# The slots stage of a twelve-stage decoder: units interleaved over three rounds, two projections merged, the fixed state's products made once

## The reference, cut to what matters

```python
S = slot_init * slot_scale                       # the same 64 x 128 state for every batch
h = gelu(concat([x, mean(S)]) @ w1.T + b1)
route_logits = (h @ w2.T + b2) / (abs(tau) + 0.1)
topk_vals, topk_idx = top_k(route_logits, 8)
alpha = one_hot(topk_idx) * softmax(topk_vals)   # tokens x 64, eight not zero
gi = (alpha.T @ x) / (alpha.sum(over tokens) + 1e-8)
xr, xz, xn = split(gi @ gru_wih.T + gru_bih); hr, hz, hn = split(S @ gru_whh.T + gru_bhh)
r, z, n = sigmoid(xr + hr), sigmoid(xz + hz), tanh(xn + r * hn)
S_new = (1 - z) * n + z * S
out = (alpha @ (S_new @ wv.T + bv)) @ wo.T + bo
```

## Time and profile before

| what | value |
|---|---|
| median of three runs | 3283.29 us (3280.67 to 3284.57) |
| the profiled execution, span | 3279.6 us |
| slots stage in it | 768.4 to 911.6 us |
| busy over the whole span | PE 83%, DVE 59%, ACT 42%, POOL 40% |

### The profile page before, as it was taken

How to read it: one execution, slowest core, us unless ns; L and a number is a source line. 1 busy time by engine, 2 the same in 40 slices (tenths; PEclk the granted TensorE clock), 3 DMA queues, 4 the chain that set the end, 5 groups by cost and what they waited for, 6 DMA issues and landing times. The chain is left out here.

```text
span 3279.6 us, 78499 instructions
## 1 busy us (share of the span) xinstructions
PE 2706.7 (83%) x31817; PEld 1927.4 (59%) x31817; DVE 1946.2 (59%) x5123; ACT 1386.3 (42%) x3116; POOL 1315.4 (40%) x1379
## 2 busy tenths in 40 slices
PE   6992566676675999799899987898979999978986
PEld 4551333344443777466799976565447777765665
DVE  6997999354554444466454444465766665645665
ACT  4552465354344555344322213554134444435544
POOL 3541566173211111444233333454643343424546
PEclk9996677787687999899799998898889999998998
DMA  3000000400000000100000000000000000000000
GB/s 104 3 2 1 1 1 1 114 1 1 1 7 33 1 2 2 41 3 3 8 1 1 1 1 4 14 2 33 12 6 2 2 2 2 2 8 2 2 2 26
DMA packets 25351, 37.33 MB, mean 11 GB/s; under 512 B 696, under 2 KB 22336, under 8 KB 24128
## 3 DMA queue, kind: packets, MB, share of 16 engines
q1 hardware_dynamic: 24992, 32.30, 3.2%
HBM read 30.07 MB, written 2.23 MB: 10 GB/s over the span
## 5 line engine op out<-in xcount | busy, mean ns | idle before, releaser
L1205 POOL TENSOR_TENSOR L_attn__qk<-L_attn__turned 128x512 f32<-128x512 f32 x128 | 161.6, 1274 | 303.5 <-DVE L_attn__turned L1316 303.5
L4316 PE MATMUL psum<-L_ffn__e_hT,weights 128*128 128x256 f32 x1024 | 245.1, 383 | 0.0
L787 DVE TENSOR_REDUCE L_xattn__nm<-psum 128x8 bf16<-128x1024 f32 x128 | 156.3, 1224 | 148.7 <-PE psum L982 142.3
L1316 DVE TENSOR_TENSOR L_attn__turned<-psum,weights 128x1024 f32<-128x1024 f32 x128 | 153.3, 1218 | 95.1 <-PE psum L1423 92.1
L4316 PEld LDWEIGHTS psum<-L_ffn__e_hT,weights 128*128 128x128 f32 x1024 | 187.0, 193 | 20.7
L4170 DVE TENSOR_TENSOR L_ffn__e_a<-L_ffn__e_sg,psum 128x512 f32<-128x512 f32 x128 | 87.9, 687 | 176.9 <-ACT L_ffn__e_sg L4162 176.8
L4162 ACT ACTIVATE L_ffn__e_sg<-psum 128x512 f32<-128x512 f32 x128 | 76.4, 597 | 259.1 <-PE psum L4316 259.1
L727 ACT ACTIVATE L_xattn__pT<-psum 128x1024 f32<-128x1024 f32 x128 | 124.0, 1021 | 58.0 <-PE psum L1010 58.0
L4329 PEld LDWEIGHTS psum<-weights,L_ffn__e_a 128*128 128x128 f32 x1024 | 134.4, 191 | 7.2 <-DVE L_ffn__e_a L4170 0.7
L1423 PE MATMUL psum<-L_attn__xT,weights 128*128 128x256 f32 x512 | 136.8, 401 | 2.0 <-DVE L_attn__turned L1316 1.3
L4329 PE MATMUL psum<-weights,L_ffn__e_a 128*128 128x128 f32 x1024 | 135.0, 275 | 0.5 <-DVE L_ffn__e_a L4170 0.5
(11 more groups left out here) (677 smaller groups left out, 7541.5 us busy)
## 6 DMA issues: line engine op xcount, KB each, us to landing
L_xattn__conv_toeplitz<-s4d_kernel SPq DMA_DIRECT2D x5, 1024.0 KB, 10.9
weights<-pack SPq DMA_DIRECT2D x1, 3328.0 KB, 10.3
weights<-pack SPq DMA_DIRECT2D x1, 3140.0 KB, 10.3
weights<-s4d_kernel SPq DMA_DIRECT2D x3, 1024.0 KB, 8.9
weights<-pack SPq DMA_DIRECT2D x1, 2370.0 KB, 9.3
out_dram<-X SPq DMA_DIRECT2D x8, 256.0 KB, 2.3
weights<-pack SPq DMA_DIRECT2D x1, 1732.5 KB, 14.4
ctxT<-ctxT_in SPq DMA_DIRECT2D x1, 1536.0 KB, 18.4
```

What stands on the lines that cost most here:

```text
L787: nc.vector.tensor_reduce(nm[:, n % 2, :].rearrange("p (g c) -> p g c", g=4)[:, 2 * u:2 * u + 2, 0:4], scores[u].rearrange("p g (i q) -> p ...
L1205: nc.gpsimd.tensor_tensor(qk[:, p % 2, u], turned[:, g % 2, :, 0:2 * P], turned[:, g % 2, :, 2 * P:4 * P], ALU.add).then_inc(qk_sb, 1)
L1316: nc.vector.tensor_tensor(turned[:, g % 2], proj[u % 2].unsqueeze(1).to_broadcast([P, 2, 4 * P]), k.w(name + "rope").rearrange("p (t q) -> ...
L4316: last = nc.tensor.matmul(bank[g % 2][:, 256 * c:256 * c + 256], k.w(name + w)[:, o:o + P], hT, start=True, stop=True)
```

## The change

Nothing outside `slots` changes but the packing of one weight (wv is stored unturned). The work is divided anew:

- The eight best of all units are chosen in the first part. sel now has a place for every unit, and `lowered` overwrites LG.
- The second part is 11 rounds; DVE does in one round the gates of unit i-1, weights of unit i+2, residual and norm of units i-2 and i-3, slot mean of unit i+1.
- The products of hsT with whh for the r and z gates, with the biases, are made once (gh_rz). DVE adds them to the accumulators in one new instruction for each unit, 128x512 (`gate_sum`, writes pre), and ACT makes th in one instruction of 128x512 from SBUF instead of two of 128x256 from PSUM.
- wv @ wo (wvo) and bv @ wo + bo are made once. `values` is one product of hnew with wvo; the svT copy is gone.
- `gather` sums over tokens with two matmuls instead of four.
- `with_bias(u)`, before the loop for unit 0, now follows `scaled` in its round.

The core of the diff:

```diff
-                pool.wait_ge(k.loaded[stage], 16)
-                with_bias(0)
-                lowered(0)
+                for u in range(UNITS):
+                    lowered(u)
                 scaled(0)
-                for v in range(UNITS + 1):
...
+                scaled(1)
+                for i in range(UNITS + 2):
+                    if unit(i - 1):
+                        difference(i - 1)
+                    if unit(i + 2):
+                        scaled(i + 2)
+                    if unit(i):
+                        with_bias(i)
+                    if unit(i - 2):
+                        root(i - 2)
...
                 def gates(u):
-                    act.wait_ge(gx_ps, u + 1)
+                    act.wait_ge(pre_sb, u + 1)
...
-                    for c in range(2):
-                        last = nc.scalar.activation(th[:, c, :], RZ[:, 4 * NS * c:4 * NS * c + 4 * NS], ACT.Tanh,
-                                                    bias=half_b[:, c:c + 1], scale=0.5)
-                    last.then_inc(th_sb, 1)
+                    nc.scalar.activation(th[:], pre[:], ACT.Tanh, scale=0.5).then_inc(th_sb, 1)
...
+                for i in range(UNITS + 3):
+                    if unit(i - 2):
+                        values(i - 2)
+                    if unit(i - 1):
+                        gates(i - 1)
+                    if unit(i):
+                        turned_mean(i)
+                    if unit(i - 1):
+                        candidate(i - 1)
+                    if unit(i - 3):
+                        block_out(i - 3)
+                    if unit(i + 1):
+                        turned_alpha(i + 1)
+                    if unit(i + 3):
+                        exponentials(i + 3)
...
+                nc.vector.tensor_copy(bv_cols[:], k.w(name + "bv").to_broadcast([P, P])).then_inc(bv_sb, 1)
...
+                def merged():
+                    dve.wait_ge(merged_ps, 1)
+                    nc.vector.tensor_copy(wvo[:], MERGED[:, 0:DM]).then_inc(merged_sb, 1)
+                    nc.vector.tensor_tensor(bo[:], MERGED[:, DM:2 * DM], k.w(name + "bo"), ALU.add).then_inc(merged_sb, 1)
...
+                def gate_sum(u):
+                    dve.wait_ge(gx_ps, u + 1)
+                    if u >= 1:
+                        dve.wait_ge(th_sb, u)
+                    nc.vector.tensor_tensor(pre[:].rearrange("p c (j n) -> p c j n", j=4),
+                                            RZ[:].rearrange("p (c j n) -> p c j n", c=2, j=4),
+                                            gh_rz[:].unsqueeze(2).to_broadcast([P, 2, 4, NS]), ALU.add).then_inc(pre_sb, 1)
...
-                        rz = RZ[:, 4 * NS * c:4 * NS * c + 4 * NS]
-                        nc.tensor.matmul(rz, k.w(name + "whh")[:, P * c:P * c + P],
-                                         hsT[:].unsqueeze(1).to_broadcast([P, 4, NS]), start=True, stop=False)
...
-                    nc.tensor.matmul(SV[:, 0:4 * NS], k.w(name + "wv"), hnew[:], start=True, stop=True).then_inc(svT_ps, 1)
-                    pe.wait_ge(svT_sb, u + 1)
...
                 gather(0)
-                for v in range(UNITS):
-                    state(v)
-                    if v + 1 < UNITS:
-                        gather(v + 1)
-                    values(v)
-                    spread(v)
+                for i in range(UNITS + 2):
+                    if unit(i):
+                        turn_mean(i)
+                    if unit(i - 2):
+                        spread(i - 2)
+                    if unit(i + 1):
+                        gather(i + 1)
+                    if unit(i):
+                        gates(i)
+                    if unit(i - 1):
+                        values(i - 1)
```

More of the change, by code:

```diff
@@ L178, in host_pack @@
     put(2, n + "bhh", g(n + "gru_bhh").reshape(3, P).T)
-    put(2, n + "wv", g(n + "wv").T)
+    put(2, n + "wv", g(n + "wv"))
     put(2, n + "bv", col(g(n + "bv")))
@@ new lines, in _ @@
+                for s in range(UNITS + 2):
+                    if s < UNITS:
+                        logits(s)
+                    if s == 0:
+                        merged()
+                    if unit(s - 2):
+                        replaced(s - 2)
+                    if unit(s - 1):
+                        best(s - 1)
+                    if unit(s - 2):
+                        selected(s - 2)
+                weighted(0)
+                weighted(1)
+                slot_mean(0)
+                for i in range(UNITS + 3):
+                    if unit(i - 1):
+                        reset_gate(i - 1)
+                    if unit(i + 2):
+                        weighted(i + 2)
+                    if unit(i - 3):
+                        shifted(i - 3)
+                    if unit(i - 2):
+                        residual(i - 2)
+                    if unit(i - 1):
+                        new_state(i - 1)
+                    if unit(i + 1):
+                        slot_mean(i + 1)
+                    if unit(i - 2):
+                        statistics(i - 2)
+                    if unit(i):
+                        gate_sum(i)
```

214 lines of the change are left out of this document (91 added, 123 removed).

## The result

The changed kernel takes 3245.66 us, median of 4 runs (3240.98 to 3249.23), against 3282.58 us before beside it (4 runs, 3280.67 to 3284.57): a ratio of 0.9889, 95% interval 0.9877 to 0.9901, or 36.9 us by the medians. A second set of runs of the same kernel gave 3242.27 us and 0.9879 (0.9863 to 0.9894). The profiled execution has a span of 3239.2 us against 3279.6.

What follows compares the result with a forecast made beforehand. The kernel was taken as bound by serial latency, then by DVE's rounds once units overlap. -43.3 + 8.6 + 1.4 - 1.8 = -35.1 us, from 3283.3, gave 3248.2 us; range 3237 to 3267.

Steps and rivals of the forecast that it cites:

- the first one: Second part of slots: DVE-bound rounds of 7.4 to 8.5 us, total 3243 to 3254 us; 60 in 100.
- a middle round: Full round of the second part, rh to next rh: 7.9 us, with DVE's 6.4 us of work and two waits.
- seven intervals: Between the eight starts of rh: 52.0 us together against 95.3, so -43.3 us.
- first part: Before the units' rounds: selection on DVE and added setup start the second part at 803.5, not 794.9: +8.6 us.
- filling: From first au to first rh: 9.75 us against 8.3, more work standing ahead of th and the gates: +1.4 us.
- tail: From last rh to the end, 13.0 us before: the svT step goes, -1.8 us.
- stage: All of slots: -43.3 + 8.6 + 1.4 - 1.8 = -35.1 us, nothing changed outside it.
- the chain is serial latency: Second part: no engine full, one unit passes all engines before the next one's gates, 13.6 us per interval.
- The fourth rival: Second part stays serial, intervals 13.6 us, total 3291.5 us; 2 in 100 slower, 3 in 100 within the band.
- the bounds around them: Pre on DVE: 0.48 us to twice that; th on ACT: 0.42 to 0.84 us.
- the prediction's layout: One full round timed from rh: hnew held by POOL's xb, ending at 4.5 not 3.7, costing 0.8 us a round.
- The power: POOL's rstd power, 1.02 us, could block DVE's rh by the skill's rule: 0.3 us a round, left out.

Runs made afterwards that it cites:

- the serial experiment: Changed kernel with the second part's loops back in the old one-unit-after-another order, all else kept: 3284.31 us, ratio 1.0006 to the kernel before.
- xb behind hnew: Changed kernel with one wait more, so POOL's xb of a round starts only after hnew of the unit before: 3238.59 us, ratio 0.9865.
- the kernel with both edits: Changed kernel with r and z gates summed in PSUM again (no gate_sum) and POOL's xb waiting for hnew: 3230.60 us, ratio 0.9843.
- the last experiment: Changed kernel with gates in PSUM, xb after hnew, bo 4 bytes on, plus 16 unused TensorE products before the first gather: 3230.24 us, ratio 0.9841.

## Why the prediction was right

**The total** came out at 3245.7 where 3248.2 was forecast, and the case was the first one, rounds bound by DVE. Term by term:

| term (us) | forecast | measured |
|---|---|---|
| a middle round | 7.9 | 7.6 to 7.8 |
| seven intervals | -43.3 | -44.6 |
| first part | +8.6 | +6.7 |
| filling | +1.4 | +3.8 |
| tail | -1.8 | -1.8 |
| stage | -35.1 | -35.9 |

The three terms that were off, by -1.3, -1.9 and +2.4 us, largely cancel: that the stage agrees to 0.8 us is in part luck. Each of the three is taken up below.

**The step of the argument that mattered, that the chain is serial latency and a second unit in flight is worth more than a shorter instruction,** is shown from both sides. The order with the selection and the two sums over tokens brings 31.3 of the 35.9 us of the stage. Everything else without the order makes the stage 5.4 us longer than before, at a granted clock of 0.54. The fourth rival, the serial chain left as it was, is what the serial experiment built: 3291.5 was forecast for it and 3284.3 measured, with intervals of 13.4 us where the rival had 13.6.

**The round's pieces.** pre was taken from r at 0.69 and took 0.66, th from an exponential of the next stage at 0.63 and took 0.63; the bounds around them were not needed. r ended 3.02 us after rh (2.94 forecast), hnew at 4.76 (4.5), mv at 6.54 (6.5), pre at 7.12 (7.2). hnew was 1.37 us where about 1.17 came out of the prediction's layout: xb itself lasts 1.38 us there and not 1.2. The place and the cause were right, as xb behind hnew showed. In the rounds without a unit to weight zd is held by xb, 1.48 us at most in its line, as foretold; the interval there was given 7.45 and measured 7.23. In the first two intervals zd was held as well, behind POOL's alpha (0.82 and 0.60 us), which the layout did not have.

**The power.** Here rows now show the two together. The power ran from 835.03 to 836.05 and rh, with two inputs in SBUF, started at 835.94 and took its usual 0.42 us. By the Trainium skill, SBUF — State Buffer, "Who interferes with whom", it should have been held until 836.05 by the instruction that issued first. xb and hnew agree with that section, this pair does not. The overlap is only 0.11 us; the kernel with both edits shows a longer one, in which au, with two inputs in SBUF too, starts 0.67 us after the power and ends before it, and takes its usual 0.41 us:

```profile
830.94 1.10 POOL L3502 TENSOR_TENSOR L_ffn__rstd<-L_ffn__rstd,neg_half 128x4 f32<-128x4 f32 x1
...
831.61 0.41 DVE L3682 TENSOR_TENSOR L_ffn__au<-L_ffn__ex,L_ffn__sel 128x256 f32<-128x256 f32 x1
```

So the 0.3 us that the prediction would have put on a round for it were rightly left out. That a 128x4 operation has read its inputs long before it ends would explain it; this was only argued.

**DVE's share** was forecast above 80% and is 53.96 of 74.2 us, 73%: filling and tail, in which it waits, are part of that window, and the forecast did not count them. In the three full rounds (828.33 to 851.37) it is 20.2 of 23.0 us, 88%, with the time that hnew is held counted as busy.

**The first part** cost 1.9 us less. The fifth logits came 0.6 us later than before, counted from the stage's start, and not 1.3: the first DVE instruction no longer stood beside xb and took 0.28 us, where it had taken 1.15, which is the "0.9 us could come back" that I had left open. From there a step of DVE took 2.13 us instead of 2.4, which I had added up from pieces whose stamps overlap a little; that is the other 1.2 us.

**The filling was the term that was mis-sized**, by 2.4 us. I had costed its products at durations of the full rounds of before. TensorE comes to it from 8.6 us without work and runs gather and gates at the 1.2 GHz level; the last experiment gives 4.4 us for that in a kernel with two products more for each unit. In the changed kernel itself it was not measured.

**One sentence of the prediction was wrong in kind,** though it did no harm to the sum: "TensorE's clock may stand where it is now without a change in the time", and with it that a product saved would be worth its time "were it on the path", 1.85 us a unit. In the serial order it was on the path, the products went, the clock fell from 0.66 to 0.54, and an interval became 0.2 us shorter.

**Outside the stage** 4.5 us more were gone in the profiled spans (3279.6 to 3239.2 is 40.4, the stage gives 35.9). The medians give 36.9. Span less stage is 3136.5 us before and 3132.0 after, both inside the 3129.6 to 3138.0 of all profiled executions, and the second trace of the changed kernel has 3135.0: the 4.5 us are within that scatter, and what makes the scatter stays open.

## What to carry to other kernels

When no engine is full and each piece starts within 0.1 us of the last one's end, put a second unit in flight before shortening any instruction; here that was 31 us and the rest of the edits together less than 5. Once it is in flight the bound can be one engine's list, as DVE's was here, and then an edit that moves work from an engine with room (two products on TensorE) onto the one that is full (an addition on DVE) can be a loss, although it saves work in sum: here 5.3 us of stage. In a chain that waits, the time of TensorE's pieces is not fixed: here fewer products ran slower by nearly as much as they were fewer, so cost them at both levels of the clock.

## What was not expected of the hardware

Unused products made a serial kernel faster: 3274.8 us with 32 more of them than the 3284.3 us without. The granted clock of the second part was 0.73 instead of 0.54.

xb, one addition on GpSimd of 128x512 with a 128x128 operand repeated four times, takes 1267 ns with that operand at one place of SBUF and 1092 when it begins 4 bytes further on. The tiles declared after it, xb's own among them, may have moved with it; which address matters was not isolated.

A power on GpSimd over 128x4, 1.02 to 1.10 us long, does not hold up a DVE instruction with two inputs in SBUF that starts 0.91 us after it, nor one that starts 0.67 us after it, while xb, 128x512, holds one to its end and 0.28 us beyond (839.04 to 840.42, hnew's end at 840.70).
